# First slots, transition and conversion order of a gated cross-attention and sparse FFN kernel on one core: turns and scores reordered, gates spread by TensorE, one mask, some loads and conversions moved

## What is computed

```python
# layernorm(v) = (v - mean) / sqrt(var + 1e-5), over the last axis
def _L0_xattn_ref(hidden_states, memory_tokens, memory_mask):
    scores = jnp.einsum('bsd,bmd->bsm', hidden_states, memory_tokens) / sqrt(512)
    scores = jnp.where(memory_mask[:, None, :], scores, -1e30)
    attn = softmax(scores)
    return where(any(memory_mask), einsum('bsm,bmd->bsd', attn, memory_tokens), 0)

def _L0_ffn_ref(x, w_gate, w_up, w_down):
    h = silu(x @ w_gate) * (x @ w_up)
    # of each 4 neighbours along the 2048, the 2 with the largest |h| stay, the rest is 0
    return _sparsify_2to4(h) @ w_down

x = x + tanh(g_xattn[0]) * _L0_xattn_ref(_layernorm(x), ctx_2048, mask_BxS2_bk0)
x = x + tanh(g_ffn[0]) * _L0_ffn_ref(_layernorm(x), w_gate, w_up, w_down)
```

## Time and profile before

| | us |
|---|---|
| median of 3 runs | 1083.94 |
| the profiled execution | 1086.38 |
| its span in the trace | 1084.6 |
| PE busy in the span | 1070.9 |
| DVE busy | 794.3 |
| ACT busy | 614.3 |
| POOL busy | 226.1 |

### The profile page before, as it was taken

The page is one execution under the profiler, slowest core; times in us unless marked ns, Lnnn a source line. Parts: engine busy times, 40 slices in busy tenths (PEclk is TensorE's granted clock), DMA queues, the critical chain, the costliest instruction groups (busy, mean ns, idle before and its releaser), DMA issues.

```text
span 1084.6 us, 15165 instructions
## 1 busy us (share of the span) xinstructions
PE 1070.9 (99%) x4972; PEld 879.4 (81%) x4972; DVE 794.3 (73%) x1389; ACT 614.3 (57%) x1126; POOL 226.1 (21%) x343
## 2 busy tenths in 40 slices
PE   7999999999999999999999999999999999999998
PEld 6888777888888888878888888878888888888887
DVE  6999879998987676676857576676856464665756
ACT  6999776777755454444544454444544444443452
POOL 7887302222111111100011111110000111111021
PEclk9999999999999999999999999999999999999999
DMA  8999985999989777787899767787798666767727
GB/s 301 323 309 323 350 355 134 329 317 289 289 268 362 174 192 189 175 271 204 241 289 285 185 177 192 180 256 203 237 306 247 153 153 155 192 151 190 199 28 144
DMA packets 89821, 252.65 MB, mean 233 GB/s; under 512 B 9104, under 2 KB 9872, under 8 KB 85648
## 3 DMA queue, kind: packets, MB, share of 16 engines
q1 hardware_dynamic: 68144, 203.45, 53.3%
q0 software_dynamic: 21600, 48.24, 26.1%
HBM read 153.09 MB, written 98.57 MB: 232 GB/s over the span
## 4 chain that ended last, share of the span: by engine, by line
PE 88%; DMA 4%; DVE 3%; ACT 2%; issue 1%; SPq 1%; POOL 0%; DVEq 0%; ACTq 0%; POOLq 0%
PE ps_y L1399 10%; PE ps_y L1401 10%; PE ps_y L1400 10%; PE ps_a L1326 9%; PE ps_a L1330 9%; PE ps_a L1328 9%; PE ps_d L1326 5%; PE ps_d L1330 5%; PE ps_d L1328 5%; PE ps_c L1353 3%; PE ps_y L1367 2%; PE ps_c L1330 2%; PE ps_c L1326 2%; PE ps_c L1328 2%; DMA x_blk<-xnT_scratch 2%; PE ps_a L1345 1%
## 5 line engine op out<-in xcount | busy, mean ns | idle before, releaser
L633 POOL DMA_DIRECT2D out_rows<-y_out x124 | 105.7, 856 | 707.5 <-ACT y_out L785 703.9
L1326 PE MATMUL ps_a<-xm,w_ring 128*128 128x512 f32 x512 | 200.2, 391 | 2.5 <-ACT cp L668 1.5
L1328 PE MATMUL ps_a<-xm,w_ring 128*128 128x512 f32 x512 | 199.6, 390 | 0.0
L1330 PE MATMUL ps_a<-xm,w_ring 128*128 128x512 f32 x512 | 199.5, 390 | 0.0
L785 ACT ACTIVATE y_out<-ps_y,ffn_gate 128x512 f32<-128x512 f32 x124 | 85.1, 688 | 182.7 <-PE ps_y L1401 182.7
L1399 PE MATMUL ps_y<-dn,h_hi 128*128 128x512 f32 x480 | 188.1, 392 | 0.3 <-ACT y_out L785 0.2
L1401 PE MATMUL ps_y<-dn,h_lo 128*128 128x512 f32 x480 | 187.2, 390 | 0.0
L1400 PE MATMUL ps_y<-dn,h_hi 128*128 128x512 f32 x480 | 186.7, 389 | 0.0
L762 ACT ACTIVATE h_hi<-hidden 128x512 fp32r<-128x512 f32 x128 | 73.2, 625 | 82.7 <-DVE hidden L1095 82.6
L1069 DVE TENSOR_TENSOR beats<-h_abs 128x512 bf16<-128x512 f32 x186 | 117.7, 684 | 1.3 <-ACT h_abs L755 1.3
L1326 PEld LDWEIGHTS ps_a<-xm,w_ring 128*128 128x128 f32 x512 | 96.1, 188 | 24.8 <-issue 3.0
(11 more groups left out here) (122 smaller groups left out, 1872.4 us busy)
## 6 DMA issues: line engine op xcount, KB each, us to landing
w_ring<-w_scratch SPq DMA_DIRECT2D x147, 512.0 KB, 4.3
out_rows<-y_out POOLq DMA_DIRECT2D x124, 256.0 KB, 4.2
w_scratch<-w_ring SPq DMA_DIRECT2D x56, 512.0 KB, 5.9
xm_scratch<-x_out SPq DMA_DIRECT2D x40, 512.0 KB, 5.5
xm<-xm_scratch SPq DMA_DIRECT2D x19, 1024.0 KB, 7.4
w_raw<-in_L_ffn_w_down SPq DMA_DIRECT2D x9, 1024.0 KB, 7.8
x_in<-in_x SPq DMA_DIRECT2D x32, 256.0 KB, 5.2
ctx_in<-in_ctx SPq DMA_DIRECT2D x32, 256.0 KB, 5.4
```

The source lines that it names most:

```text
L633: nc.gpsimd.dma_start(out[RING * (n // (2 * TILES * QS)) + TILES * ORDER[order] + n % TILES], y_out[:, n % 4], accum_op=ALU.add).then_inc( ...
L1326: nc.tensor.matmul(to, w_ring[:, k, e, 0, c], xm[:, k, 0, c], start=begins and c == 0, stop=False, skip_group_check=not begins)
L1328: nc.tensor.matmul(to, w_ring[:, k, e, 0, c], xm[:, k, 1, c], start=False, stop=False, skip_group_check=not begins)
L1330: last = nc.tensor.matmul(to, w_ring[:, k, e, 1, c], xm[:, k, 0, c], start=False, stop=c == 1, skip_group_check=not begins)
```

## The change

- **PE, first slots.** The slots 0 to 2 are written out: turn ctx 0, turn x 0, turn ctx 1, score 0, turn x 1, turn ctx 2, score 1, turn x 2. Before, score 0 stood behind turn x 1, and score 1 behind turn x 2. PE then spreads the two gates over the partitions with one matmul of a row of ones (2 columns), and the multiplication of block 1 waits for both gates.
- **Gates.** They are loaded as two numbers on one partition, by ACT's DMA queue, at the start; before, by SP as a broadcast to 128 partitions, between the loads of block 4 and its mask. ACT's tanh reads PSUM.
- **Masks.** The mask bytes get a place of their own in memory (that of the last x operand), the fourth mask is loaded in slot 14 and converted in slot 21 instead of 7, and the wait for it moves from the ninth copy of x1nT to `x_high` (0, 6).
- **Tables.** PIECE_AT, SPREAD_AT: some entries one slot later, (1, 0) and (1, 1) later. X0_AT: the eight operands i = 3 to 6 are made in slots 30 to 37 instead of 29 to 36. The last two low parts are made by DVE behind `add_c11` of unit 0; before, POOL made the first of them and DVE the other, in slot 37.
- **SP, end of the slots.** The load of piece (2, 1) and of x_blk stand behind the last store of xnT; before, in front of it.
- **ACT, second stage.** Unit 1: both `copy_a1` before the four `dn_high`, then `copy_d0`, `spread(2, 3)`, `x_high_at`. Step 1: `copy_d0` before a spread and `x_high_at`. Later steps: `copy_d0` before `x_high_at(s, 0)`.
- **DVE, second stage.** Unit 0: `gated0` of a tile straight behind its `add_c12`. Steps after 4: `x_low_at(s, 0)` behind `add_c22`.

```diff
-CONVERT = {1: 0, 3: 1, 4: 2, 7: 3}
+CONVERT = {1: 0, 3: 1, 4: 2, 21: 3}
-PIECE_AT = {6: (0, 2), 7: (0, 3), 11: (1, 0), 12: (1, 1), 28: (1, 2), 29: (1, 3), 36: (2, 0), 37: (2, 1)}
-SPREAD_AT = {5: ((0, 0),), 6: ((0, 1),), 10: ((0, 2),), 11: ((0, 3),), 21: ((1, 0),), 22: ((1, 1),)}
+PIECE_AT = {6: (0, 2), 8: (0, 3), 12: (1, 0), 13: (1, 1), 28: (1, 2), 30: (1, 3), 36: (2, 0)}
+SPREAD_AT = {5: ((0, 0),), 7: ((0, 1),), 10: ((0, 2),), 11: ((0, 3),), 22: ((1, 0),), 29: ((1, 1),)}
-         | {29 + 2 * (i - 3) + k: (k, i) for i in range(3, 7) for k in range(2)})
+         | {30 + 2 * (i - 3) + k: (k, i) for i in range(3, 7) for k in range(2)})
...
+        mask_in = Place((PROD - 1) * 4 * 4 * HALF)("mask_in", [P, B * M], U8, 1)
...
-                if n == SLOTS - 3:
-                    load_x_blk(sp, 1, 0)
+            load_w_piece(sp, nc.sync, 2, 1)
+            load_x_blk(sp, 1, 0)
...
+            for n, g in enumerate((g_xattn, g_ffn)):
+                nc.scalar.dma_start(gates_in[:, n:n + 1], g.rearrange("(a n) -> a n", a=1)).then_inc(gates_loaded, 16)
...
-                        act.wait_ge(gates_loaded, 32)
-                        nc.scalar.activation(xattn_gate[:], gates_in[:, 0:1], ACT.Tanh).then_inc(gates_done, 1)
+                        act.wait_ge(gates_spread, 1)
+                        nc.scalar.activation(xattn_gate[:], ps_av[1][:, 0:1], ACT.Tanh).then_inc(gates_done, 1)
...
                         copy_a1(u, 1)
-                        x_high_at(s, 0)
                         copy_d0(u, 0)
                         copy_d0(u, 1)
+                        x_high_at(s, 0)
...
-                    dn_high(0, 0)
-                    dn_high(0, 1)
                     copy_a1(1, 0)
                     copy_a1(1, 1)
-                    dn_high(0, 2)
-                    dn_high(0, 3)
-                    x_high_at(0, 1)
-                    spread(act, 2, 3)
+                    for j in range(GROUP):
+                        dn_high(0, j)
                     copy_d0(1, 0)
                     copy_d0(1, 1)
+                    spread(act, 2, 3)
+                    x_high_at(0, 1)
...
-                    if s > QS:
-                        x_low_at(s, 0)
                     add_c22(u, 0)
                     add_c22(u, 1)
                     if s <= QS:
                         dn_low(dve, nc.vector, s - 1)
-                        x_low_at(s, 0)
+                    x_low_at(s, 0)
...
+                    dve.wait_ge(x_lo_done, 12)
+                    x_low(dve, nc.vector, 0, 0, 6)
+                    x_low(dve, nc.vector, 0, 1, 6)
...
                     add_c12(0, 0)
+                    gated0(0, 0)
                     add_c12(0, 1)
+                    gated0(0, 1)
                     w_low(dve, nc.vector, 1, 5)
-                    gated0(0, 0)
-                    gated0(0, 1)
...
+            turn_ctx(0)
+            turn_x(0)
+            turn_ctx(1)
+            score(0)
+            turn_x(1)
+            turn_ctx(2)
+            score(1)
+            turn_x(2)
+            pe.wait_ge(ones_set, 1)
+            pe.wait_ge(gates_loaded, 32)
+            nc.tensor.matmul(ps_av[1][:, 0:2], ones[:], gates_in[:], start=True, stop=True).then_inc(gates_spread, 1)
+            for n in range(3, SLOTS):
+                if 3 < n <= B:
+                    turn_ctx(n - 1)
+                    turn_x(n - 1)
+                if 3 < n < B + 2:
+                    score(n - 2)
```

More of the change, by code:

```diff
@@ L479, in _ @@
                     load_mask(0)
[L480 to L483, removed]
                 if b in (4, 5):
@@ L710, in _ @@
                     if b == 0:
-                        act.wait_ge(gates_loaded, 32)
-                        nc.scalar.activation(xattn_gate[:], gates_in[:, 0:1], ACT.Tanh).then_inc(gates_done, 1)
-                        nc.scalar.activation(ffn_gate[:], gates_in[:, 1:2], ACT.Tanh).then_inc(gates_done, 1)
+                        act.wait_ge(gates_spread, 1)
+                        nc.scalar.activation(xattn_gate[:], ps_av[1][:, 0:1], ACT.Tanh).then_inc(gates_done, 1)
+                        nc.scalar.activation(ffn_gate[:], ps_av[1][:, 1:2], ACT.Tanh).then_inc(gates_done, 1)
                     act.wait_ge(pT_done, b + 1)
@@ L722, in _ @@
                 if n in X0_AT:
+                    if X0_AT[n] == (0, 6):
+                        act.wait_ge(mask_neg_done, B // RING)
                     x_high(act, 0, *X0_AT[n])
@@ L932, in _ @@
                     copy_a1(u, 1)
+                if s == 1:
+                    copy_d0(u, 0)
+                    copy_d0(u, 1)
                 if building:
@@ L938, in _ @@
                 x_high_at(s, 2)
-                copy_d0(u, 0)
-                copy_d0(u, 1)
+                if s > 1:
+                    copy_d0(u, 0)
+                    copy_d0(u, 1)
                 if building:
@@ L996, in _ @@
                         x_sum(dve, 0, *X0_AT[n])
-                if n == SLOTS - 2:
-                    dve.wait_ge(x_lo_done, 13)
-                    x_low(dve, nc.vector, 0, *X0_AT[n - 1])
                 b = n - 3
@@ L1332, in product @@
                 last.then_inc(made[k], 1)
-            for n in range(SLOTS):
-                b = n - 1
-                if 0 <= b < B:
-                    pe.wait_ge(ctx_in_loaded[b % INPUTS], 16 * (b // INPUTS + 1))
-                    wait(pe, cT_copied, b)
-                    for c in range(KC):
-                        last = nc.tensor.transpose(ps_cT[:, c], ctx_in[:, b % INPUTS, c * P:(c + 1) * P], ident[:])
-                    last.then_inc(cT_done, 1)
-                    pe.wait_ge(xn_done, b + 1)
-                    wait(pe, xT_copied, b)
-                    for c in range(KC):
-                        last = nc.tensor.transpose(ps_xT[:, c], xn[:, b % 2, c * P:(c + 1) * P], ident[:])
-                    last.then_inc(xT_done, 1)
-                b = n - 2
-                if 0 <= b < B:
-                    pe.wait_ge(xT_copied, b + 1)
-                    pe.wait_ge(cT_copied, b + 1)
-                    wait(pe, neg_scores_done, b - 1)
-                    for c in range(KC):
-                        last = nc.tensor.matmul(ps_sc[b % 2][:, 0:M], xnT[:, b % 2, c], ctxT[:, b % 2, c],
-                                                start=(c == 0), stop=(c == KC - 1))
-                    last.then_inc(scores_done, 1)
@@ new lines, in turn_ctx, with turn_x @@
+            def turn_ctx(b):
+                pe.wait_ge(ctx_in_loaded[b % INPUTS], 16 * (b // INPUTS + 1))
+                wait(pe, cT_copied, b)
+                for c in range(KC):
+                    last = nc.tensor.transpose(ps_cT[:, c], ctx_in[:, b % INPUTS, c * P:(c + 1) * P], ident[:])
+                last.then_inc(cT_done, 1)
+            def turn_x(b):
+                pe.wait_ge(xn_done, b + 1)
+                wait(pe, xT_copied, b)
+                for c in range(KC):
+                    last = nc.tensor.transpose(ps_xT[:, c], xn[:, b % 2, c * P:(c + 1) * P], ident[:])
+                last.then_inc(xT_done, 1)
@@ new lines, in score @@
+            def score(b):
+                pe.wait_ge(xT_copied, b + 1)
+                pe.wait_ge(cT_copied, b + 1)
+                wait(pe, neg_scores_done, b - 1)
+                for c in range(KC):
+                    last = nc.tensor.matmul(ps_sc[b % 2][:, 0:M], xnT[:, b % 2, c], ctxT[:, b % 2, c],
+                                            start=(c == 0), stop=(c == KC - 1))
+                last.then_inc(scores_done, 1)
+            turn_ctx(0)
+            turn_x(0)
+            turn_ctx(1)
```

14 lines of the change are left out of this document (8 added, 6 removed).

## The result

The changed kernel takes **1088.81 us** (median of 5, 1088.33 to 1091.03); the kernel before, beside it, 1084.35 (1083.72 to 1085.29). The ratio is 1.0041, 95% interval 1.0029 to 1.0054: slower by 4.5 us, above the range that ended at 1084.5. The profiled execution of after took 1088.81 us, span 1086.9, against 1086.38 and 1084.6 for the one of before, so the two traces show only 2.4 of the 4.5.

The account below looks back on a forecast made before the run. PE was taken as the bound (1070.9 of 1084.6 us). The terms 0.45 - 0.95 + 0.57 + 0.33 + 1.05 gave 1.45 us gained, taking the median from 1083.94 to 1082.5 us, range 1080.3 to 1084.5.

Parts of the forecast that it names:

- The steps between had no gap; x_high later by 1.0 has slack there: 0: Late steps other than 6 and 10: ACT's x_high 1.0 us later was to cost nothing.
- four rivals: Transition's list starts at once, 1081.0 (0.23); no slot-36 wait, 1081.5 (0.08); slow clock, 1083.6 (0.16); late x_blk, 1086.2 (0.08).
- x_blk late in the transition: Rival: ACT waits in x_high_at(0, 0) for x_blk with its copies behind, 1086.2 us; chance 0.08.
- Slot 36: Product k=2 of unit 0 waits for POOL's low part of operand (1, 5): 0.95 us lost.
- Transition: Units 0 to 2: gaps at copies go, PE waits for DVE at k=6 and unit 2 instead: 0.57 us gained.
- First slots: Score 0 fills PE's gap before turn x 1, full rate comes at about 11.4 us: 0.45 us gained.
- Step 1: Unit 3: copy_d0 before spread and x_high removes a 0.54 gap, k=6 late by about 0.2: 0.33 us gained.
- Steps 6 and 10: Gap at k=5 goes, PE waits longer at the copy of y: 0.5 and 0.55, together 1.05 us gained.

Follow-up runs that it names:

- f7: Kernel before with one edit: ACT's copy_d0 ahead of x_high_at(s, 0) for s > 1; 1086.20 us, ratio 1.0012.
- e4: Kernel before with one edit: from step QS+1 on DVE makes the low part and sum of x behind add_c22; 1088.38 us, ratio 1.0034.
- c0: Kernel before, unchanged, run again; 1085.29 us, ratio 1.0009.
- h1: Kernel before plus 14 idle turns of the identity by PE, nine before the first ctx turn, five between ctx 0 and x 0; 1084.74 us, ratio 0.9998.
- h2: f1 plus the same 14 idle turns of the identity as h1; 1084.38 us, ratio 0.9994.
- c1: Kernel before, unchanged, run a third time; 1084.17 us, ratio 0.9993.
- e1: Changed kernel with DVE's x_low_at(s, 0) in front of add_c22 again in steps after 4; 1086.13 us, ratio 1.0015.
- f1: Changed kernel with DVE's x_low in front of add_c22 again and X0_AT one slot earlier again; 1084.62 us, ratio 1.0000.
- f2: Changed kernel with x_low in front of add_c22, X0_AT one slot earlier and score 0 behind turn x 1 again; 1085.45 us, ratio 1.0008.
- f3: f2 with SP's loads of weight piece (2, 1) in slot 37 and x_blk in slot SLOTS-3 again; 1088.15 us, ratio 1.0036.
- f6: f2 with copy_d0 of unit 3 behind spread and x_high again; 1084.83 us, ratio 1.0003.
- g1: f1 repeated, unchanged; 1085.95 us, ratio 1.0015.

## Why the prediction was wrong, step by step

- **The step that failed** is "The steps between had no gap; x_high later by 1.0 has slack there: 0". It priced ACT's move and forgot the other half of the edit, DVE's x_low_at behind `add_c22` for every step after 4. In steps 6 and 10 that wait was looked at; in 7 and 11 the pair had been filling 1.3 us of DVE's wait for PE, and what follows is a row of DVE without a hole on which ACT's copy of y hangs, and PE on that. Forecast 0, measured 2.4 in steps 7 and 11 in the traces (2.2 over all of stretch C). The slack that it gave ACT's move wasn't there either: f7 shows 0.5 for both steps together, a cost that DVE's covers when both moves are made (2.4 in e4 too). None of the four rivals was this one; the slower one chosen (x_blk late in the transition) did not occur: ACT began its part at 136.0, after a wait for DVE, not for x_blk.
- **Slot 36**: right in kind and size. Forecast 0.95, traced 1.0 at the spot and 0.91 in stretch B. The one difference is that the row names "issue" and not POOL.
- **Transition**: right in size, and in the place of the new gaps. 0.57 forecast; stretch B says 0.5 (62.91 less 62.43), with the gaps moved to k=6 of unit 1 and to unit 2 as forecast. ACT's list started its spread at 138.79 and not at 137.5, for weight piece (2, 2) and not for x_blk. (The list as forecast adds up to 147.2 and not 147.3, which changes nothing.)
- **First slots**: the term of 0.45 was wrong, because it took the moment at which PE's rate rises from one trace and moved it with PE's work. Before and c0, and h1 and h2, show that it does not follow from that. In 18 traces A runs from 107.24 to 109.47. The seven with score 0 ahead of turn x 1 mean 108.38, the eleven with it behind 108.49; the eleven with the new loads, masks and gates mean 108.51, the seven without 108.35. The moves there are worth nothing measurable, beside 1.4 us between two executions of one kernel.
- **Step 1**: mis-sized. Forecast 0.33, traced 0.16, as a gap at the copy of y near 211 was not foreseen.
- **Steps 6 and 10**: mis-sized. Forecast 1.05. In these two steps together PE stands still for 2.2 us in the first trace of before, 2.0, 1.2 and 1.5 in c0, c1 and h1, and 1.6 in after: a gain of 0.6 by the first trace and of 0.1 by the mean of the four. The gap that one trace showed was a late landing of x_blk, present in step 6 in two of the four, and the longer gap at the copy of y (0.69 for 0.41) comes from DVE's pair, for which the forecast had no term here either: e4 has it too. Without the pair the seven kernels e1, f1, f2, f3, f6, g1 and h2 have 0.8 to 2.2, mean 1.3, so 0.4 is gained there, and steps 7 and 11 take 0.5 back.
- **The sum of what the traces show**: A +0.2, slot 36 +1.0, transition -0.5, steps 7 and 11 +2.4, steps 6 and 10 -0.1, step 1 -0.2: 2.8 us, where a gain of 1.45 was forecast. The medians say 4.5. The profiled executions of before (1086.38, 1085.16, 1085.00) lie up to 2 us above most of its medians, and single times of it reach down to 1082.5; of those no trace exists, so 1.7 us stay unexplained. Undoing x_low and X0_AT together (f1, g1) brings the time to 1.0000 and 1.0015 of before, so the two costs account for 2.8 to 4.4 of the 4.4 us; neither f1 nor any other kernel is faster than before by a measurable amount.

## What to carry over

When an operation is moved behind a wait, ask first what the engine did during that wait: two operations of 0.6 us cost nothing in front of `add_c22` and 1.2 us behind it, since the row that follows has no hole up to the operation on which PE's next wait hangs. An edit under a condition such as `s > QS` has to be costed in every step that it reaches, above all in those that show no gap now. And a gap that rests on a DMA's landing should be seen in a second execution before its removal is counted as a gain.

## What the hardware showed that I had not expected

- PE's full rate at the start came at 14.1 us in the first trace of before and at about 10.5 in c0, the same kernel; it came by 6.8 in h2 and behind 12.7 in h1, with the same 14 turns of the identity ahead. The granted clock read 1.00 in all windows of h1 and h2 from 4 to 16 us. In h1:

```profile
8.00:12.00 4.00, 3.47 (x17) 3.07 (x16) 1.53 (x5) 2.96 (x5) 2.58 (x7) 1.00 1.03 306
```

  Only the duration of the turns (1.1 or 0.6 us for four) tells the level of 1.2 or 2.4 GHz there. The Trainium skill, TensorE: Matmul & The Clock Gate ("What you observe"), says of matmuls back to back that the place of this change varies by some half microsecond between runs. Here, where PE waits in between, two executions of one kernel were 3.5 us apart, so for this start the measurement decides.
- In the middle of the kernel a wait of PE of 2.1 us was followed by matmuls 0.43 us apart, the 1.2 GHz level, up to 215.15, eight of them in 3.4 us (g1), so a load that came 2 us late cost 3.6. A wait of the same length in f3, at 148.11, was followed by matmuls 0.23 us apart; the runs don't show what makes the difference.
- A 512 KB weight piece took 7.9 us from issue to use in one execution and 9.9 in another, at the same place.
- Repeats of one kernel's text, on two chips, had medians 1.3 us apart (f1 and g1), with intervals of about 1 us either way that only just meet.
